# A six-layer-norm decoder stack: tiles 0 to 3 of each layer norm are transposed at the end of the stage before

## The reference, cut to what matters

```
x = layernorm(x + L0_attn(x))           # A: 32 heads of 16, alibi bias
x = layernorm(x + L0_xattn(x, ctx, ctx))# B: 32 query heads on 8 key heads of 128, rope, mask
x = layernorm(x + L0_ffn(x))            # C: dense + 8 low-rank experts, top 2
x = layernorm(x + L1_attn(x))           # D: 32 query heads on 8 key heads of 128, causal window of 64
x = layernorm(x + L1_xattn(x, ctx))     # E: one head of 512 against ctx
x = layernorm(x + L1_ffn(x))            # F: gate, up, down with 16-level weights and low-rank parts
layernorm(x): (x - mean(x)) / sqrt(var(x) + 1e-5) over the 512 features
```

## Time and profile before

| | |
|---|---|
| median of 3 runs | 1708.49 us |
| profiled execution | 1707.01 us |
| its span, first to last instruction | 1705.2 us |
| TensorE matmul busy | 1596.9 us (94%) |
| VectorE, ScalarE, GpSimd busy | 983.1, 659.7, 202.9 us |
| mean granted TensorE clock | 0.979 |

### The profile page before, as it was taken

The page is one execution under the profiler, slowest core; times in us unless marked ns, Lnnn a source line. Parts: engine busy times, 40 slices in busy tenths (PEclk is TensorE's granted clock), DMA queues, the critical chain, the costliest instruction groups (busy, mean ns, idle before and its releaser), DMA issues. The chain is left out here.

```text
span 1705.2 us, 22804 instructions
## 1 busy us (share of the span) xinstructions
PE 1596.9 (94%) x8526; PEld 1277.1 (75%) x8526; DVE 983.1 (58%) x1946; ACT 659.7 (39%) x1191; POOL 202.9 (12%) x146
## 2 busy tenths in 40 slices
PE   8788689999999999999889999999999999979998
PEld 6565477788778778876777788788878877757866
DVE  5897757756676676667433542552553446246645
ACT  4666424433443443334333332332332323336541
POOL 8421130000000000000340000000000000703330
PEclk9999899999999999999999999999999999999999
DMA  5110011100110110100111110110110100202221
GB/s 211 50 44 26 15 48 38 62 26 27 50 50 1 51 62 13 38 13 26 45 51 38 38 50 9 53 52 10 49 62 12 37 13 25 79 6 83 77 80 50
DMA packets 26023, 75.44 MB, mean 44 GB/s; under 512 B 3888, under 2 KB 4624, under 8 KB 25680
## 3 DMA queue, kind: packets, MB, share of 16 engines
q1 hardware_dynamic: 25552, 73.16, 12.9%
q0 software_dynamic: 384, 1.05, 0.2%
HBM read 72.10 MB, written 2.10 MB: 44 GB/s over the span
## 5 line engine op out<-in xcount | busy, mean ns | idle before, releaser
L83 PE MATMUL bankY<-sb_Dwo,sb_DoT 128*128 128x512 f32 x768 | 193.4, 401 | 0.3 <-DVE sb_DoT L1033 0.3
L83 PE MATMUL bankY<-sb_Bwo,sb_BoT 128*128 128x512 f32 x768 | 193.3, 401 | 0.2 <-DVE sb_BoT L1033 0.2
L83 PE MATMUL bankA<-sb_xT,sb_Bwq 128*128 128x512 f32 x768 | 190.1, 397 | 0.0
L83 PE MATMUL bankA<-sb_xT,sb_Dwq 128*128 128x512 f32 x768 | 189.9, 396 | 0.0
L83 PEld LDWEIGHTS bankY<-sb_Dwo,sb_DoT 128*128 128x128 f32 x768 | 140.6, 189 | 42.4 <-issue 13.6
L83 PEld LDWEIGHTS bankY<-sb_Bwo,sb_BoT 128*128 128x128 f32 x768 | 140.8, 189 | 42.1 <-issue 13.2
L83 PEld LDWEIGHTS bankA<-sb_xT,sb_Dwq 128*128 128x128 f32 x768 | 142.2, 188 | 34.1 <-issue 2.7
L83 PEld LDWEIGHTS bankA<-sb_xT,sb_Bwq 128*128 128x128 f32 x768 | 142.3, 188 | 33.7 <-issue 2.4
L964 DVE TENSOR_TENSOR sb_BqT<-bankA,sb_Btable 128x512 f32<-128x512 f32 x64 | 44.2, 691 | 151.6 <-ACT sb_Bsw L866 151.6
L1000 DVE TENSOR_TENSOR sb_xtok<-sb_xtok,bankY 128x512 f32<-128x512 f32 x128 | 87.1, 680 | 53.7 <-PE bankY L83 53.6
L866 ACT ACTIVATE sb_Bsw<-bankA 64x512 f32<-64x512 f32 x160 | 94.8, 593 | 54.8 <-PE bankA L83 51.7
(11 more groups left out here) (277 smaller groups left out, 2987.1 us busy)
## 6 DMA issues: line engine op xcount, KB each, us to landing
sb_raw<-in_w_attn SPq DMA_DIRECT2D x80, 512.0 KB, 3.4
sb_raw<-in_q_gu SPq DMA_DIRECT2D x22, 256.0 KB, 2.7
sb_raw<-in_q_d SPq DMA_DIRECT2D x11, 256.0 KB, 2.7
sb_rawx<-in_xT SPq DMA_DIRECT2D x4, 512.0 KB, 6.5
sb_raw<-in_wqk SPq DMA_DIRECT2D x8, 256.0 KB, 2.6
sb_xtok<-in_x_tok SPq DMA_DIRECT2D x1, 2048.0 KB, 11.9
sb_raw<-in_ctxT SPq DMA_DIRECT2D x4, 512.0 KB, 3.8
sb_raw<-in_ctx_tok SPq DMA_DIRECT2D x4, 512.0 KB, 3.8
```

The lines of the kernel that those rows point to most:

```text
L83: last = nc.tensor.matmul(out, lhs, rhs, start=start and i == 0, stop=stop and i == len(pairs) - 1)
```

## The change

The transposes of tiles 0 to 3 of norms 0 to 4 are issued at the end of the block before (`EARLY`), those of tiles 4 to 7 stay at the start of the next. Eight places in PSUM are used: tiles 0 and 1 in T0 and T1, 2 and 3 in A0 and A1, 4 and 5 in Y0 and Y1, 6 and 7 in T0 and T1 again. In B and D the copies out of the banks (high and low part) of tiles 0 to 3 are also made in the last unit; so C and E begin with tile 4. After A, C and E they stay at the start of the next block. In B and D ScalarE now scales tiles 0 to 3 in unit 14, and VectorE waits for the root of that group at tile 4.

```diff
-    ln_banks = [bankT[0], bankT[1], bankY[0], bankY[1]]
+    ln_banks = [bankT[0], bankT[1], bankA[0], bankA[1], bankY[0], bankY[1], bankT[0], bankT[1]]
+    EARLY = range(4)
...
-    def ln_tensor(pe, n):
-        for t in range(NT):
+    def ln_tensor(pe, n, tiles=range(4, NT)):
+        for t in tiles:
             wait_normalised(pe, n, t)
-            if t >= 4:
-                pe.wait_ge(ln_low, n * NT + t - 3)
+            if t >= 6:
+                pe.wait_ge(ln_low, n * NT + t - 5)
             for k in range(KC):
-                done = nc.tensor.transpose(ln_banks[t % 4][:, k * P:(k + 1) * P], xtok[:, t, k * P:(k + 1) * P], ident[:])
+                done = nc.tensor.transpose(ln_banks[t][:, k * P:(k + 1) * P], xtok[:, t, k * P:(k + 1) * P], ident[:])
             done.then_inc(ln_tr, 1)
...  # A, tensor, the last line
                 output_last(NT - 1)
+                ln_tensor(pe, 0, EARLY)
...  # B and D, the the waits of D's first products
-                            tiles = {"V": 2 * n + 2, "K": ...
+                            tiles = {"V": max(2 * n + 2, 4), "K": ...
...  # B and D, tensor
                             done.then_inc(o_ready, 1)
+                            if part.final and u == SLOTS - 1:
+                                ln_tensor(pe, norm + 1, EARLY)
...  # B and D, scalar
                             if part.final and u == SLOTS - 2:
                                 ln_roots(act, norm + 1, 0)
+                                ln_scale(act, norm + 1, 0)
                             if part.final and u == SLOTS - 1:
-                                ln_rest(act, norm + 1)
+                                ln_high_parts(act, norm + 1, EARLY)
+                                ln_roots(act, norm + 1, 1)
+                                ln_scale(act, norm + 1, 1)
+                                ln_roots(act, norm + 1, 2)
+                                ln_scale(act, norm + 1, 2)
...  # B and D, vector
-                            ln_follow(dve, norm + 1, t)
+                            ln_follow(dve, norm + 1, t, early=1)
...
+                            if part.final and u == SLOTS - 1:
+                                ln_low_parts(dve, norm + 1, EARLY)
                             if u % NT == NT - 1:
                                 residual(part, u - 1)
...  # C and E, tensor, the last lines
+                ln_tensor(pe, 2, EARLY)
+                ln_tensor(pe, 4, EARLY)
...  # C and E, scalar and vector, the first lines
-                ln_high_parts(act, 1)
+                ln_high_parts(act, 1, range(4, NT))
-                ln_low_parts(dve, 1)
+                ln_low_parts(dve, 1, range(4, NT))
```

More of the change, by code:

```diff
@@ L147, in ln_follow, with ln_low_parts, ln_high_parts @@
             nc.vector.tensor_scalar(xtok[:, t, :], xtok[:, t, :], rstd[:, t:t + 1], offset[:, t:t + 1], ALU.mult, ALU.add).then_inc(ln_last, 1)
-    def ln_low_parts(dve, n):
-        for t in range(NT):
+    def ln_low_parts(dve, n, tiles=range(NT)):
+        for t in tiles:
             dve.wait_ge(ln_high, n * NT + t + 1)
-            nc.vector.tensor_tensor(xT[1][:, :, t * P:(t + 1) * P], ln_banks[t % 4][:].rearrange("p (k c) -> p k c", k=KC),
+            nc.vector.tensor_tensor(xT[1][:, :, t * P:(t + 1) * P], ln_banks[t][:].rearrange("p (k c) -> p k c", k=KC),
                                     f32(xT[0][:, :, t * P:(t + 1) * P]), ALU.subtract).then_inc(ln_low, 1)
-    def ln_high_parts(act, n):
-        for t in range(NT):
+    def ln_high_parts(act, n, tiles=range(NT)):
+        for t in tiles:
             act.wait_ge(ln_tr, n * NT + t + 1)
             nc.scalar.activation(xT[0][:, :, t * P:(t + 1) * P],
-                                 ln_banks[t % 4][:].rearrange("p (k c) -> p k c", k=KC), ACT.Copy).then_inc(ln_high, 1)
-    def ln_tensor(pe, n):
-        for t in range(NT):
+                                 ln_banks[t][:].rearrange("p (k c) -> p k c", k=KC), ACT.Copy).then_inc(ln_high, 1)
+    def ln_tensor(pe, n, tiles=range(4, NT)):
+        for t in tiles:
             wait_normalised(pe, n, t)
-            if t >= 4:
-                pe.wait_ge(ln_low, n * NT + t - 3)
+            if t >= 6:
+                pe.wait_ge(ln_low, n * NT + t - 5)
             for k in range(KC):
-                done = nc.tensor.transpose(ln_banks[t % 4][:, k * P:(k + 1) * P], xtok[:, t, k * P:(k + 1) * P], ident[:])
+                done = nc.tensor.transpose(ln_banks[t][:, k * P:(k + 1) * P], xtok[:, t, k * P:(k + 1) * P], ident[:])
             done.then_inc(ln_tr, 1)
@@ L759, in project @@
                         if part.order is START and not (rope and kind in "KV"):
-                            tiles = {"V": 2 * n + 2, "K": NT // 2 * (n % 2 + 1), "Q": NT // 2 * (n // 4 + 1), "S": NT // 2}[kind]
+                            tiles = {"V": max(2 * n + 2, 4), "K": NT // 2 * (n % 2 + 1), "Q": NT // 2 * (n // 4 + 1), "S": NT // 2}[kind]
                             pe.wait_ge(ln_low, norm * NT + tiles)
@@ L1262, in _ @@
                     product(bankY[t % 2][:], three([p[:, t, :] for p in pT], [f[:, t, :] for f in ft])).then_inc(y_ready, 1)
+                ln_tensor(pe, 4, EARLY)
             @block.scalar
             def _(act):
-                ln_high_parts(act, 3)
+                ln_high_parts(act, 3, range(4, NT))
                 act.wait_ge(small, 32)
@@ L1283, in _ @@
             def _(dve):
-                ln_low_parts(dve, 3)
+                ln_low_parts(dve, 3, range(4, NT))
                 dve.wait_ge(small, 32)
```

## The result

The changed kernel takes 1715.45 us (median of 7 runs, 1711.95 to 1717.16), the kernel before 1708.75 in the same session (7 runs, 1707.74 to 1709.88). The ratio is 1.0038, with an interval of 1.0026 to 1.0050: slower, by 6.7 us. The forecast was 1713.5 us on 1708.49, +5.0. The profiled execution took 1715.45 us with a span of 1713.7; that of before had a span of 1705.2. So the spans differ by 8.5 us, but 1.66 of it is there at A's last outputs, which lie ahead of the first instruction that the change touches. I count such a piece as the scatter of single executions; 6.8 us are left for the change.

What follows compares the result with a forecast made beforehand. TensorE, with a matmul in flight for 94% of the span, was taken to bound the kernel. B's start -2.0, ends +11.2, C, E, D -1.9 -1.8 -1.0, F -1.3, holes +1.8 gave +5.0 on 1708.49: 1713.5 us, range 1709.0 to 1718.0.

Steps and rivals of the forecast that it cites:

- The ends of B and D: Before output(15): attend(15) 3.3 us late, then 2.3 for transposes and half clock; +5.6 each, +11.2 together.
- The rival of a clock held through the hole: Clock stays up before attend(15) in B and D; each end +3.5, total 1706.4 us; chance 0.08.
- C, D and E up to the first product: First product starts 4.4 us after the start, when POOL's first split ends: -1.9, -1.0 and -1.8 us.
- The holes: In C, D and E, TensorE idle about 1 us before the product delays the clock: +0.6 each, +1.8.
- late-clock rival: The hole in C, D and E costs its upper bound, 5.7 instead of 1.8: 1717.4 us; chance 0.18.
- B's start: VectorE reaches the table copies earlier, after its eight low parts: -2.2, net -2.0 us with A's end.
- F: At F's start, 16 transposes left: product 1.8 us earlier, less 0.5 for half clock, so -1.3.
- Its own test of the starts: Prediction wrong if the starts together give back under 5 or over 9 us.
- attend(15) less than 3 us late: At the ends of B and D: would show the prediction wrong; 3.3 us late was expected.
- outputs at full clock throughout: At the ends of B and D: a sign that would show the prediction wrong.
- The early-clock rival: Clock rises 2.7 us after each restart; ends 4.7 each, holes 0: +2.0, 1710.5 us; chance 0.27.
- the one of the transposes that don't bring the clock up: At ends and starts, the rise comes 4.5 us after outputs or products start: +15.5, 1724 us; chance 0.02.

Runs made afterwards that it cites:

- filled kernel: Changed kernel plus identity transposes as filler between the transposes and the first product, 8 in C and E, 5 in D: 1708.95 us, ratio 1.0004.
- fourth experiment: Changed kernel, but in B and D the transposes come after output(15), scaling stays in unit 15, copies move to the next start: 1699.72 us, ratio 0.9956.
- held kernel: The fourth experiment with tile 3's four transposes repeated six and five more times at the ends of C and E: 1698.23 us, ratio 0.9937.

## Why the prediction was right, and where it was off

**The ends of B and D: right in each step.** Predicted 3.3 + 2.3 each, measured 3.37 + 2.37 and 3.37 + 2.38, together 11.5 instead of 11.2. The idle time before attend(15), the order behind it, and the clock at 0.50 over the transposes are in the timeline and the windows after. The early scaling alone reproduces the 5.58 us of idleness; the transposes alone were not run at this place, so their 1.4 to 1.8 is a difference of two kernels. The rise came 4.8 us after attend(15), the estimate was 4.5. The rival of a clock held through the hole is out: 0.50 stood behind all eight holes of 5.58 us in the traces.

**C, D and E up to the first product: right.** -1.9, -1.0 and -1.8 predicted; -1.90, -0.96 and -1.80 measured, with POOL's split as what ends the wait.

**The holes: the mis-sized term, +1.8 against +5.3.** The step was "I don't take nothing: +0.6 each", between bounds of 0 and 1.9. Measured were 1.68, 2.01 and 1.64, at the upper bound, and this is the late-clock rival's mechanism (5.7). The prediction took a third of the bound, while its nearest row, a start busy for 5.7 us still at 0.50, spoke for more. What the row could not tell, and the filled kernel with F's starts shows, is that the hole matters and not the number of transposes. D's 2.01 is a little above the bound because its clock rose 4.5 us into the product and not 4.

**B's start: mis-sized the other way, -2.0 against -3.94.** The step "VectorE comes to them after its eight low parts" left out the two mask instructions between, which the description of the kernel before names. The low parts came early as predicted (8 of them from 209.65 to 214.53); then the two took 4.1 us together instead of 5.7, which the run with GpSimd held back traces to GpSimd.

**F: -1.3 predicted, -1.23 measured, as -2.04 and +0.81.** The predicted path was another: here the clock was still up at F's start (transposes of 1.06 us for eight), fell at 1548.5, under them, and rose at 1551.9, 1.9 us into the product. The sum is right and the way to it is not.

**Its own test of the starts came out against it.** The prediction called itself wrong if the starts together give back under 5 or over 9 us. With the losses behind the holes they gave back 4.5 us (6.2 predicted), without them 9.8 (8.0 predicted): outside on either count. Of the other two signs, attend(15) less than 3 us late did not show; outputs at full clock throughout is no test, since the prediction's own sum has them so, and they ran at 0.50 only for their first 0.3 us (1456.06 to 1456.4). One of the things to look for failed as well: the wait of L734 was to be some 2 us shorter and was 0.6 shorter.

**The sum.** The two errors, +3.5 in the holes and -1.9 in B, make +1.6, and the ends +0.3: with F +0.1 and -0.15 that went nowhere, +5.0 becomes +6.8. Two errors of opposite sign made the total look better than its parts; that the time lies in the range is to that extent luck. The early-clock rival (+2.0) asked for holes that cost nothing and is out; the one of the transposes that don't bring the clock up (+15.5) is out too. The Trainium skill, TensorE: Matmul & The Clock Gate, Part 4: PE-mode transpose, says that transposes don't bring the clock up as matmuls do. For these fp32 transposes the traces disagree again: at F's start in the filled kernel nothing but 16 transposes runs behind 3.29 us of idleness, at 0.50, and the clock is at 1.00 from 1540.9, before the product begins at 1541.12. (A's end in the changed kernel shows less: 1.4 us of output matmuls ran at 0.50 ahead of the transposes there.)

**Open.** After a start without a hole the clock rose 2.7 to 5.8 us behind the first transpose, in C for instance 5.8 in the kernel before and with GpSimd held back, but 3.2 with the scaling alone, though C's own start is the same in all three. The scaling alone gained its 0.90 us in C there: 32 transposes in 5.4 us instead of 6.3. In the kernel before and in the one with GpSimd held back C, D, E and F repeat within 0.1 us, so it seems to hang on what came before; but B's end in the fourth experiment and in the held kernel, with the same program ahead, had the clock up in one and down in the other. On what it hangs exactly, no experiment here settles.

## What to carry to other kernels

Before work is put in front of the instruction that an engine is waiting for, ask whether it could stand behind it: the 16 transposes with their early scaling cost 5.7 us at each end ahead of the last outputs, and behind them, with the scaling left where it was, nothing; the whole change went from 6.7 us slower to 7.1 faster by that and by what it does behind, a clock that stays up at C's and E's starts. A start that is made shorter only up to what another engine allows leaves a hole, and where the clock is down a hole of 0.8 to 1.8 us gives back most of what it had saved, or more (1.68 of 1.90 us, 1.64 of 1.80, 2.01 on 0.96); fill it, or keep the clock from falling. When a stall's end is an instruction in one engine's list, read every instruction of that list between the step moved and the stall, and what its neighbour engine does beside each.

## What the runs showed of the hardware that I had not expected

- With the clock at 0.50, a hole of 0.8 to 1.8 us between transposes and product moved the rise from 2.7 to 5.8 us after the first transpose to 7.8 to 9.0.
- The clock can fall after TensorE has restarted: at F's start in the changed kernel at 1548.5, 1.7 us behind the first transpose, after 3.29 us of idleness; at C's and E's 1.1 us behind it, after 3.55; in D of the held kernel 1.4 us into a product.
- A hole of 2.21 us in full work was followed by 0.50 at 11 ends and by 1.00 at three, in two of the kernels with the same program up to there.
- A VectorE instruction on 1024 columns of int32 took 0.68 us with GpSimd still, and 1.32, 2.37, 2.82 or 3.40 beside its splits and its memset.
